# Attention order in steps of two: scores, transposes and applied probabilities of neighbouring steps stand together on PE, with new orders on ACT and DVE

## Chip, core and metric

The kernel runs on one core of a Trainium2 chip. The metric is the device time of one execution in microseconds. It is one program with two blocks: an attention layer (until about 1140 us) and an expert layer behind it.

## What is computed

x holds 64 graphs of 128 nodes with 512 features, adj a 128 x 128 matrix for each. The attention layer has 16 heads of 32 features; adj is used twice as the bias.

```python
h = jnp.maximum(_layernorm(x, axis=-1), 0.0)
x = x + _L0_gnn_ref(h, adj, adj, Wq, Wk, Wv, Wo)
# _L0: q, k, v = split_heads(h @ Wq.T), (h @ Wk.T), (h @ Wv.T)
#      a = einsum('bhnd,bhmd->bhnm', q, k) * 512**-0.5 + 2 * adj
#      p = softmax(a)   (rows that are all zero give p = 0)
#      o = einsum('bhnm,bhmd->bhnd', p, v);  return o @ Wo.T
h = jnp.maximum(_layernorm(x, axis=-1), 0.0)
x = x + _L1_gnn_ref(h, adj, router_w, router_b, expert_w, bn_gamma, bn_beta)
```

The change touches the attention layer alone.

## The kernel before

The attention layer works on two graphs at a time (a pair, 32 pairs). Each graph's 16 heads are four steps of four heads, so a pair has the steps 0 to 7. Every product is made exact in three terms (hi times hi, hi times lo, lo times hi), which is why an operand is copied by ACT (hi) and then subtracted by DVE (lo).

Each engine has an order written out by hand as a string of tokens (`PE_ORDER`, `ACT_ORDER`, `DVE_ORDER`, `POOL_ORDER`, `SP_ORDER`). One pass over the strings is one turn of the loop; a turn starts one S0 after the other. A token is a letter and a step or part. A prime means the pair before; `AHEAD` moves some letters one or two pairs ahead. An engine works strictly in the order of its string and waits at a token for semaphores. The tokens that matter here:

- S: four score matmuls of a step on PE (line 420). L: the scaled scores plus bias, and the negated row maximum, on DVE (lines 356, 361). E: four exponentials on ACT (line 301). B: maximum of the absolute values on DVE (line 364). R: reciprocal and norm on DVE (lines 369, 372). P: the scaling by the norm on POOL (line 268). T: four transposes on PE (line 427). C: their copy on ACT (line 308). W: eight matmuls, 32 columns of weights each, that apply the probabilities on PE (line 436).
- Q0 to Q3: the projections of the next pair on queries (0, 1) and keys (2, 3): 24 matmuls each on PE (line 461, recorded at 43), the copy on ACT (line 319), the subtraction on DVE (line 387). V0, V1: the values, and their copy on ACT (line 325). H: transposes of the normalised input. O: the output projection, with a copy on ACT (line 312) and a subtraction on DVE (line 377). X: the residual on DVE. N and M: layer norm statistics. A: the normalisation on ACT.
- K0 and K1 on the SP queue (lines 244 to 252): 12 transfers each, of 128 KB, that put the queries and keys of a pair's first and second graph from `qk` into `stack`. K0 waits for the last subtraction Q3 of the pair. K1 stands as K1' in the next turn, behind Y1' (a store of 256 KB) and X (a load of 512 KB) in the same queue. Nothing in SP's order is changed.
- `qk` exists once. So ACT's copy Q0 of the next pair waits until all 24 transfers of the pair before have landed:

```python
                        wait(act, qk_projected, 4 * j + k + 1)
                        if k == 0:
                            for g in range(2):
                                wait(act, stacked[g], STACKS * j)
```

S0 waits for K0's landing, S4 for K1's. W0 waits for the subtraction O1' (`o_split`). `bank` has three PSUM banks that Q, V, O and H share by `Q_BANK`, `V_BANK`, `O_BANK` and `H_BANK`; who writes a bank waits until its last reader is done.

Of the kernel before, what the change touches and what calls it, by code (L numbers as in the profile page):

```python
# [32 lines left out]
def wait(engine, semaphore, value):  # L33

    if not isinstance(value, int) or value > 0:
        engine.wait_ge(semaphore, value)
# [31 lines left out]
def attention_layer(nc, ctx, sem, ident, x, adj, weights, x1_dram, expert_w, shared):  # L68
# [14 lines left out]
    def ps(name, shape):  # L83
# [45 lines left out]
    h_transposed, hT_hi_ready, hT_split = sem("h_transposed"), sem("hT_hi_ready"), sem("hT_split")  # L129
    qk_projected, qk_hi_ready, qk_split = sem("qk_projected"), sem("qk_hi_ready"), sem("qk_split")  # L130
    stacked = [sem("stacked0"), sem("stacked1")]
    v_projected, v_copied = sem("v_projected"), sem("v_copied")
# [7 lines left out]
    x1_ready = sem("x1_ready")  # L140
# [5 lines left out]

    PE_ORDER = """S0 W5' T6' H1' O0'
                  S1 T7' W6' Q0  # L150
                  S2 T0 W7' Q1
                  S3 T1 W0 Q2
                  S4 W1 T2 Q3
                  S5 T3 W2 O1'
                  S6 T4 W3 V0
                  S7 T5 W4 H0 V1"""

    ACT_ORDER = """H1' C6' E0
                   C7' E1
                   C0 Q0 O1' E2  # L160
                   V1' Q1 C1 E3
                   Q2 C2 E4
                   Q3 C3 E5
                   C4 A0 O0 E6
                   A1 V0 C5 H0 E7"""

    DVE_ORDER = """R7' L0 H1' B0
                   N0 R0 L1 X0' B1
                   N1 L2 R1 Q0 O1' B2
                   R2 L3 Q1 B3  # L170
                   M R3 L4 Q2 B4
                   R4 Q3 L5 B5
                   L6 R5 X1' B6
                   O0 R6 L7 H0 B7"""

    POOL_ORDER = "P7' D1' P0 P1 P2 P3 G P4 D0 P5 P6"

# [8 lines left out]
             ("sp", PAIRS - 1): "K1' F Z1' Y0' Z0 Y1'",  # L186
             ("act", PAIRS): "C6' F0 C7' O1' F1", ("dve", PAIRS): "R7' F0 X0' O1' X1' F1"}

    Q_BANK, V_BANK, O_BANK, H_BANK = (2, 1, 0, 2), (2, 0), (1, 1), (1, 2)

    def tokens(engine, order, i):

        for t in (START.get((engine, i), order) if isinstance(i, int) else order).split():
            pair = 0 if t[0] in "UF" else i + (AHEAD[engine].get(t[0], 0) - t.endswith("'"))
            if not isinstance(pair, int) or 0 <= pair < PAIRS:
                yield t[0], int(t[1:].strip("'") or 0), pair
# [16 lines left out]
    with nc.Block() as block:  # L213
# [71 lines left out]
        def _(act):  # L285
            def body(i):
                for token, k, j in tokens("act", ACT_ORDER, i):
                    slot = k % 4
# [50 lines left out]
        def _(dve):  # L339
            def body(i):  # L340
                for token, k, j in tokens("dve", DVE_ORDER, i):
                    slot = k % 4
# [67 lines left out]
        @block.tensor  # L410
        def _(pe):
            def body(i):
                for token, k, j in tokens("pe", PE_ORDER, i):
                    g, c, slot = k // C, k % C, k % 4
                    if token == "S":
                        if c == 0:
                            wait(pe, stacked[g], STACKS * (j + 1))
                        wait(pe, logits_ready, STEPS * j + k - 1)
                        for r in range(R):
                            last = nc.tensor.matmul(scores_ps[:, k % 2, r], stack[:, g, r, 0, c], stack[:, g, r, 1, c],  # L420
                                                    start=True, stop=True)
                        last.then_inc(scored, 1)
                    elif token == "T":
                        wait(pe, normed, STEPS * j + k + 1)
                        wait(pe, probT_ready, STEPS * j + k - 1)
                        for r in range(R):
                            last = nc.tensor.transpose(probT_ps[:, k % 2, r], prob[:, slot, r], ident[:])  # L427
                        last.then_inc(transposed, 1)
                    elif token == "W":
                        wait(pe, probT_ready, STEPS * j + k + 1)  # L430
                        if c == 0:
                            wait(pe, v_copied, 2 * j + g + 1)
                            wait(pe, o_split, 2 * j + g)
                        for r in range(R):
                            f = HD * (R * c + r)
                            last = nc.tensor.matmul(o_ps[HD * r:HD * r + HD, c], v[:, g, f:f + HD], probT[:, slot, r],  # L436
                                                    start=True, stop=True)
                        last.then_inc(applied, 1)
                    elif token == "O":
                        wait(pe, o_split, 2 * j + k + 1)  # L440
                        if isinstance(j, int) and j == 0 and k == 0:
                            pe.wait_ge(w_split, 4)

                        if exists(j + 2):
                            wait(pe, *((hT_split, 2 * (j + 2) + 1), (qk_split, 4 * (j + 2) + 2))[k])
                        else:
                            wait(pe, x1_ready, 2 * j + k)
                        exact_product(nc, bank[:, O_BANK[k]], [o_hi[:, c] for c in range(C)], [o_lo[:, c] for c in range(C)],
                                      [w_hi[:, 3, c] for c in range(C)], [w_lo[:, 3, c] for c in range(C)]
                                      ).then_inc(o_projected, 1)  # L450
                    elif token == "Q":
                        if isinstance(j, int) and j == 0 and k % 2 == 0:
                            pe.wait_ge(w_split, k // 2 + 1)

                        wait(pe, *((hT_split, 2 * (j + 1)), (x1_ready, 2 * (j - 2) + 1), (v_copied, 2 * j),
                                   (qk_split, 4 * j + 1))[k])
                        for half in range(2):
                            m = 128 * (2 * (k % 2) + half)
                            last = exact_product(nc, bank[:, Q_BANK[k], 256 * half:256 * half + 256],
                                                 [w_hi[:, k // 2, kc, m:m + 128] for kc in range(KC)],  # L460
                                                 [w_lo[:, k // 2, kc, m:m + 128] for kc in range(KC)],
                                                 [hT_hi[:, kc] for kc in range(KC)], [hT_lo[:, kc] for kc in range(KC)])
                        last.then_inc(qk_projected, 1)
                    elif token == "V":
                        if isinstance(j, int) and j == 0 and k == 0:
                            pe.wait_ge(w_split, 3)
                        wait(pe, qk_split, 4 * j + (4, 3)[k])
                        exact_product(nc, bank[:, V_BANK[k]], [hT_hi[:, kc, k] for kc in range(KC)],
                                      [hT_lo[:, kc, k] for kc in range(KC)],
                                      [w_hi[:, 2, kc] for kc in range(KC)], [w_lo[:, 2, kc] for kc in range(KC)]  # L470
                                      ).then_inc(v_projected, 1)
                    elif token == "H":
                        wait(pe, h_ready, 2 * j + k + 1)

                        wait(pe, *((x1_ready, 2 * (j - 2)), (v_copied, 2 * (j - 1) + 1))[k])
                        for kc in range(KC):
                            last = nc.tensor.transpose(bank[:, H_BANK[k], 128 * kc:128 * kc + 128],
                                                       h[:, k, 128 * kc:128 * kc + 128], ident[:])
                        last.then_inc(h_transposed, 1)

            keep_clock_up(nc, pe, bank[:, 0, 0:128], ident, 40)
            run(pe, body)


def expert_layer(nc, ctx, sem, ident, x1_dram, adj, router_w, router_b, gamma, beta, out_dram, y, shared):
# [83 lines left out]

    PE_ORDER = "Z0 Z1 J P0 P1 Z2 P2 Z3 P3 M"  # L570
    ACT_ORDER = "A2' A3' Z0 P0 A0 A1 Z1 P1 Z2 P2 Z3 P3"
    DVE_ORDER = "M' Y0 Y1 S3' N0 Z0 S0 Z1 S1 Y2 N1 Z2 S2 Y3 J Z3"
    POOL_ORDER = "N0 P0 N1 P1 P2 P3"
# [70 lines left out]
    with nc.Block() as block:  # L644
# [96 lines left out]
        def _(act):  # L741
            def body(i, stays):
                for token, g, group in tokens("act", ACT_ORDER, i):
                    n = G * group + g
# [36 lines left out]
        def _(dve):  # L781
# [18 lines left out]
            def body(i, stays):  # L800
                for token, g, group in tokens("dve", DVE_ORDER, i):
                    n = G * group + g
# [114 lines left out]
        def _(pe):  # L917
            def body(i, stays):
                for token, g, group in tokens("pe", PE_ORDER, i):
                    n = G * group + g  # L920
# [134 lines left out]
```

## Time and profile before

| | |
|---|---|
| median of 3 runs | 1625.91 us (1625.65 to 1627.64) |
| span of the profiled execution | 1624.5 us |
| PE busy | 1414.4 us, 87% |
| weight loads | 1211.5 us, 75% |
| DVE busy | 1220.7 us, 75% |
| ACT busy | 931.5 us, 57% |
| POOL busy | 539.8 us, 33% |
| SP's queue q1 | 218.20 MB, 51.7% of 16 engines |

The shares are means over the span. The slices of the profile show PE at 9 tenths in all slices of the attention layer but the first and the last, DMA between 5 and 6 tenths there, and DVE alone in the last three slices, after the expert layer's matmuls. A wait is named by what came last before it, so a wait that appears rarely and briefly can still be one that is nearly due in each turn.

### The profile page before, as it was taken

How to read it: one execution, taken by the hardware profiler on the slowest of the kernel's cores; microseconds unless marked ns; L12 is line 12 of the kernel's file. 1: busy time of each engine (PE TensorE's matmuls, PEld its weight loads, DVE VectorE, ACT ScalarE, POOL GpSimd, SP SyncE). 2: the span in 40 equal slices, each digit the busy share in tenths (PEclk: the TensorE clock that was granted, in tenths of full speed). 3: DMA queues.
4: the chain of work that ended last, by engine and by line, in shares of the span. 5: the costliest groups of instructions: out<-in, count | busy, mean ns of one | idle time of the engine just before them, and what ended most of it. 6: DMA issues, size and time to landing. Idle time of an engine off the chain costs nothing. (4 is left out here: it accounts for less than half of the span.)

```text
span 1624.5 us, 38099 instructions
## 1 busy us (share of the span) xinstructions
PE 1414.4 (87%) x10994; PEld 1211.5 (75%) x10995; DVE 1220.7 (75%) x2645; ACT 931.5 (57%) x2957; POOL 539.8 (33%) x593
## 2 busy tenths in 40 slices
PE   7999999999999999999999999998799999982000
PEld 6888888888888888888888888886577777772000
DVE  4777777777777777777777777776676667758998
ACT  4677676676766766766766766766455454520000
POOL 0222222223232232222232232222234344425655
PEclk9999999999999999999999999998799999996555
DMA  5955566655666545666555666545243322127963
GB/s 185 249 135 123 135 150 155 151 126 119 147 154 154 142 119 128 150 156 147 137 119 139 151 155 149 123 108 143 92 144 129 129 96 80 46 72 269 342 228 124
DMA packets 144864, 235.52 MB, mean 145 GB/s; under 512 B 17842, under 2 KB 34226, under 8 KB 144818
## 3 DMA queue, kind: packets, MB, share of 16 engines
q1 hardware_dynamic: 136370, 218.20, 51.7%
q10 hardware_dynamic: 8448, 16.78, 2.8%
q8 instruction: 21, 0.34, 0.1%
q14 instruction: 25, 0.20, 0.0%
HBM read 92.30 MB, written 41.94 MB: 83 GB/s over the span
## 5 line engine op out<-in xcount | busy, mean ns | idle before, releaser
L268 POOL TENSOR_TENSOR prob<-prob,norm 128x512 f32<-128x512 f32 x256 | 266.7, 1042 | 789.2 <-DVE norm L372 789.2
L301 ACT ACTIVATE prob<-logits,neg_max 128x128 f32<-128x128 f32 x1024 | 398.1, 394 | 70.0 <-DVE neg_max L361 69.9
L43 PE MATMUL bank<-hT_hi,w_hi 128*128 128x256 f32 x1024 | 303.6, 296 | 2.8 <-DVE hT_lo L405 2.5
L43 PE MATMUL bank<-hT_lo,w_hi 128*128 128x256 f32 x1024 | 291.3, 284 | 0.0
L43 PE MATMUL bank<-hT_hi,w_lo 128*128 128x256 f32 x1024 | 291.1, 284 | 0.0
L356 DVE SCALAR_TENSOR_TENSOR logits<-scores_ps,adj 128x512 f32<-128x512 f32 x256 | 176.7, 690 | 133.6 <-PE scores_ps L420 132.7
L308 ACT ACTIVATE probT<-probT_ps 128x512 f32<-128x512 f32 x256 | 152.7, 596 | 143.0 <-PE probT_ps L427 143.0
L43 PEld LDWEIGHTS bank<-hT_hi,w_hi 128*128 128x128 f32 x1024 | 197.2, 193 | 21.4 <-issue 19.2
L43 PEld LDWEIGHTS bank<-hT_lo,w_hi 128*128 128x128 f32 x1024 | 197.8, 193 | 0.0
L43 PEld LDWEIGHTS bank<-hT_hi,w_lo 128*128 128x128 f32 x1024 | 197.4, 193 | 0.0
L301 ACT ACTIVATION_READ_ACCUMULATOR prob<-logits,neg_max 128x1 f32 x1024 | 195.5, 191 | 0.0
L361 DVE TENSOR_REDUCE neg_max<-logits 128x4 f32<-128x512 f32 x256 | 175.7, 686 | 8.7
L364 DVE TENSOR_REDUCE abs_max<-logits 128x4 f32<-128x512 f32 x256 | 172.9, 676 | 0.0
L427 PE MATMUL probT_ps<-ident,prob 128*128 128x128 f32 x1024 | 163.6, 283 | 4.6 <-POOL prob L268 4.4
L420 PEld LDWEIGHTS scores_ps<-stack 96*128 96x128 f32 x1024 | 146.2, 193 | 16.3 <-DMA stack<-qk 5.6
L420 PE MATMUL scores_ps<-stack 96*128 96x128 f32 x1024 | 145.1, 265 | 4.7 <-DMA stack<-qk 4.7
L43 PE MATMUL out_ps<-w_hi,z_hi 128*128 x256 | 106.8, 417 | 22.2 <-issue 13.4
L427 PEld LDWEIGHTS probT_ps<-ident,prob 128*128 128x128 f32 x1024 | 108.6, 142 | 18.3 <-issue 12.7
L764 ACT ACTIVATE z_hi<-z_ps 128x512 fp32r<-128x512 f32 x64 | 38.1, 598 | 139.1 <-PE out_ps L43 135.0
L736 POOL TENSOR_TENSOR outs<-outs,h x64 | 94.2, 1476 | 58.7 <-DVE outs L904 58.7
L387 DVE TENSOR_TENSOR qk<-bank,qk 128x512 fp32r<-128x512 f32 x128 | 87.8, 686 | 32.2 <-ACT qk L319 32.1
L436 PE MATMUL o_ps<-probT,v 128*32 128x128 f32 x2048 | 109.7, 286 | 0.8 <-ACT probT L308 0.3
(127 smaller groups left out, 2875.2 us busy)
## 6 DMA issues: line engine op xcount, KB each, us to landing
stack<-qk SPq DMA_DIRECT2D x768, 128.0 KB, 2.5
x_in<-in_x SPq DMA_DIRECT2D x32, 512.0 KB, 4.7
x_res<-in_x SPq DMA_DIRECT2D x64, 256.0 KB, 2.8
x_dram<-x_res SPq DMA_DIRECT2D x64, 256.0 KB, 2.8
x_in<-x_dram SPq DMA_DIRECT2D x32, 512.0 KB, 3.7
y<-outs ACTq DMA_DIRECT2D x16, 1024.0 KB, 5.2
out_dram<-outs SPq DMA_DIRECT2D x32, 256.0 KB, 2.0
w_hi<-x_dram SPq DMA_DIRECT2D x8, 1024.0 KB, 9.6
```

What stands on the lines that cost most here:

```text
L43: last = nc.tensor.matmul(out, a, b, start=(n == 0), stop=(n == len(terms) - 1))
L268: nc.gpsimd.tensor_tensor(prob[:, slot], prob[:, slot], norm[:, slot].unsqueeze(2).to_broadcast([N, R, N]), ALU.mult).then_inc(normed, 1)
L301: last = nc.scalar.activation(prob[:, slot, r], logits[:, slot, r], ACT.Exp, bias=neg_max[:, slot, r:r + 1], accum_out=row_sum[:, slot, r: ...
L308: nc.scalar.activation(probT[:, slot], probT_ps[:, k % 2], ACT.Copy).then_inc(probT_ready, 1)
L356: nc.vector.scalar_tensor_tensor(out=logits[:, slot], in0=scores_ps[:, k % 2], scalar=SCALE, in1=adj2[:, k // C].unsqueeze(1).to_broadcast ...
L361: nc.vector.tensor_reduce(neg_max[:, slot], logits[:, slot], X, ALU.max, negate=True).then_inc(neg_max_ready, 1)
L364: nc.vector.tensor_reduce(abs_max[:, slot], logits[:, slot], X, ALU.max, apply_absolute_value=True).then_inc(abs_max_ready, 1)
L387: nc.vector.tensor_tensor(qk[:, lo, :, c:c + 2].rearrange("p g c n -> p c g n"), bank[:, Q_BANK[k]].rearrange("p (c g n) -> p c g n", c=2, ...
L420: last = nc.tensor.matmul(scores_ps[:, k % 2, r], stack[:, g, r, 0, c], stack[:, g, r, 1, c], start=True, stop=True)
L427: last = nc.tensor.transpose(probT_ps[:, k % 2, r], prob[:, slot, r], ident[:])
L436: last = nc.tensor.matmul(o_ps[HD * r:HD * r + HD, c], v[:, g, f:f + HD], probT[:, slot, r], start=True, stop=True)
L736: nc.gpsimd.tensor_tensor(out, out, coef_rows[1][:, bass.ds(e, 1)], ALU.add).then_inc(shifted, 1)
```

## The change

The orders of PE, ACT and DVE in the attention layer are rewritten. On PE two S stand together, then two T and two W of earlier steps; before, each S, T and W stood alone between larger blocks. Q2 and Q3 swap their banks (2 and 0 instead of 0 and 2), and the waits of Q2, Q3, V0 and V1 follow. POOL's and SP's orders, the unrolled orders at the start and the end, and all instructions stay.

```diff
-    PE_ORDER = """S0 W5' T6' H1' O0'
-                  S1 T7' W6' Q0
-                  S2 T0 W7' Q1
-                  S3 T1 W0 Q2
-                  S4 W1 T2 Q3
-                  S5 T3 W2 O1'
-                  S6 T4 W3 V0
-                  S7 T5 W4 H0 V1"""
-
-    ACT_ORDER = """H1' C6' E0
-                   C7' E1
-                   C0 Q0 O1' E2
-                   V1' Q1 C1 E3
-                   Q2 C2 E4
-                   Q3 C3 E5
-                   C4 A0 O0 E6
-                   A1 V0 C5 H0 E7"""
-
-    DVE_ORDER = """R7' L0 H1' B0
-                   N0 R0 L1 X0' B1
-                   N1 L2 R1 Q0 O1' B2
-                   R2 L3 Q1 B3
-                   M R3 L4 Q2 B4
-                   R4 Q3 L5 B5
-                   L6 R5 X1' B6
-                   O0 R6 L7 H0 B7"""
+    PE_ORDER = """S0 S1 H1' O0' T6' T7' W4' W5' Q0
+                  S2 S3 Q1 T0 T1 W6' W7' Q2
+                  S4 S5 Q3 T2 T3 W0 W1 O1'
+                  S6 S7 V0 T4 T5 W2 W3 H0 V1"""
+
+    ACT_ORDER = """H1' E0 C6' E1 C7'
+                   Q0 E2 Q1 C0 E3 C1 O1' V1'
+                   Q2 E4 Q3 C2 E5 C3
+                   A0 A1 E6 C4 E7 O0 H0 V0 C5"""
+
+    DVE_ORDER = """R7' L0 L1 H1' B0 R0 X0' B1 N0 R1
+                   Q0 L2 L3 B2 R2 Q1 B3 N1 R3
+                   Q2 L4 L5 O1' B4 R4 Q3 M B5 R5
+                   L6 L7 X1' B6 R6 B7 O0 H0"""
...
-    Q_BANK, V_BANK, O_BANK, H_BANK = (2, 1, 0, 2), (2, 0), (1, 1), (1, 2)
+    Q_BANK, V_BANK, O_BANK, H_BANK = (2, 1, 2, 0), (2, 0), (1, 1), (1, 2)
...
-                        wait(pe, *((hT_split, 2 * (j + 1)), (x1_ready, 2 * (j - 2) + 1), (v_copied, 2 * j),
-                                   (qk_split, 4 * j + 1))[k])
+                        wait(pe, *((hT_split, 2 * (j + 1)), (x1_ready, 2 * (j - 2) + 1), (qk_split, 4 * j + 1),
+                                   (v_copied, 2 * j))[k])
...
-                        wait(pe, qk_split, 4 * j + (4, 3)[k])
+                        wait(pe, qk_split, 4 * j + (3, 4)[k])
```

## Rows read from the trace of the kernel before

**Rows 1.** Busy time by stretch: engines with counts, granted clock, DMA share, GB/s.
```profile
80.00:1160.00 1080.00, 1067.78 (x8596) 916.73 (x8594) 817.84 (x1832) 743.85 (x2587) 309.45 (x377) 0.99 0.58 138
1116.00:1124.00 8.00, 7.63 (x46) 5.43 (x47) 5.34 (x14) 5.94 (x24) 2.45 (x4) 0.50 0.50 157
1200.00:1260.00 60.00, 55.12 (x410) 45.93 (x408) 41.37 (x124) 30.10 (x54) 27.18 (x29) 1.00 0.37 127
```

**Rows 2.** Timeline of SP's queue: start, length, line, transfers, count, merged.
```profile
612.47 7.70 SPq L249 DMA_DIRECT2D stack<-qk  x12
...
646.94 7.70 SPq L249 DMA_DIRECT2D stack<-qk  x12
...
656.43 7.69 SPq L249 DMA_DIRECT2D stack<-qk  x12
...
681.42 7.68 SPq L249 DMA_DIRECT2D stack<-qk  x12
...
716.08 7.68 SPq L249 DMA_DIRECT2D stack<-qk  x12
```

**Rows 3.** Timeline of ACT: copy Q0 in two turns; in brackets the wait.
```profile
634.65 0.60 ACT L319 ACTIVATE qk<-bank 128x512 fp32r<-128x512 f32 x1 [0.45 <-DMA stack<-qk]
...
704.11 0.60 ACT L319 ACTIVATE qk<-bank 128x512 fp32r<-128x512 f32 x1 [0.96 <-DMA stack<-qk]
```

**Rows 4.** DMA issues, 663.3 to 664.1: count, KB each, us to landing.
```profile
stack<-qk SPq DMA_DIRECT2D x2, 128.0 KB, 4.0
```

**Rows 5.** What copies of line 319 waited for, 400 to 1100: us, times.
```profile
  DMA stack<-qk: 2.7, 5
```

**Rows 6.** Timeline of ACT, 635 to 640, first instructions of E, V1', Q1, E.
```profile
635.63 0.41 ACT L301 ACTIVATE prob<-logits,neg_max 128x128 f32<-128x128 f32 x1
...
637.17 0.58 ACT L325 ACTIVATE v<-bank 128x512 f32<-128x512 f32 x1
637.65 0.59 ACT L319 ACTIVATE qk<-bank 128x512 fp32r<-128x512 f32 x1
...
639.13 0.40 ACT L301 ACTIVATE prob<-logits,neg_max 128x128 f32<-128x128 f32 x1 [0.41 <-DVE neg_max L361]
```

**Rows 7.** Timeline of DVE, 635 to 647: Q, O, R, L, Q and Q3.
```profile
635.28 0.69 DVE L387 TENSOR_TENSOR qk<-bank,qk 128x512 fp32r<-128x512 f32 x1 [0.36 <-ACT qk L319]
635.89 0.68 DVE L377 TENSOR_TENSOR o_lo<-o_ps,o_hi 128x512 fp32r<-128x512 f32 x1
...
637.30 0.18 DVE L369 RECIPROCAL inv_sum<-row_sum 128x4 f32<-128x4 f32 x1
...
637.68 0.69 DVE L356 SCALAR_TENSOR_TENSOR logits<-scores_ps,adj 128x512 f32<-128x512 f32 x1
...
639.01 0.68 DVE L387 TENSOR_TENSOR qk<-bank,qk 128x512 fp32r<-128x512 f32 x1
...
646.14 0.69 DVE L387 TENSOR_TENSOR qk<-bank,qk 128x512 fp32r<-128x512 f32 x1 [0.86 <-ACT qk L319]
```

**Rows 8.** Timeline of PE, 602 to 609: groups S, T, W and first Q matmuls.
```profile
602.35 0.56 PE L420 MATMUL scores_ps<-stack 96*128 96x128 f32 x4
602.74 0.62 PE L427 MATMUL probT_ps<-ident,prob 128*128 128x128 f32 x4
603.29 0.43 PE L436 MATMUL o_ps<-probT,v 128*32 128x128 f32 x8
603.65 0.38 PE L43 MATMUL bank<-hT_hi,w_hi 128*128 128x256 f32 x1
603.87 0.28 PE L43 MATMUL bank<-hT_lo,w_hi 128*128 128x256 f32 x1
...
606.62 0.56 PE L420 MATMUL scores_ps<-stack 96*128 96x128 f32 x4
...
607.46 0.66 PE L427 MATMUL probT_ps<-ident,prob 128*128 128x128 f32 x4
607.88 0.36 PE L43 MATMUL bank<-hT_hi,w_hi 128*128 128x256 f32 x1
```

## The prediction

> **What bounds the kernel now.** I read the busy time by stretch first. Between 80 and 1160 us PE is busy 1067.8 of 1080 us at the full clock, so in the attention layer PE is the bound and nobody else is: DVE has 817.8, ACT 743.9 [rows 1]. The turns are equal: K0's first transfer is issued at 612.47 and again at 646.94, that is 34.47 us per turn [rows 2]. One turn is one pair. 29 turns are of this full kind; the first, the last two and the expert layer are other stretches.
>
> A busy PE is only half of the reading. The second question is what is nearly late. ACT's copy Q0 carries a bracket "<-DMA stack<-qk", 0.45 us in one turn and 0.96 us in another [rows 3]; there were 5 such waits, 2.7 us in all, in the 20 turns from 400 to 1100 [rows 5]. So the transfers of K1 land about when ACT comes to Q0, and there is a second loop beside PE's: K0 and K1 issued, landed, Q0 copied, the chain of ACT and DVE up to the subtraction Q3, K0 issued again.
>
> Its first half is the transfers. K0's 12 issues take 7.70 us, 0.64 each; K1's first comes 9.49 us after K0's first (646.94 to 656.43), as Y1' and X stand between, and takes 7.69 again [rows 2]. The last issue is near 663.5 and lands 4.0 later [rows 4], at 667.5: 20.6 after K0's start. In the turns in which ACT waited, it started 22.18 (612.47 to 634.65) and 22.69 (681.42 to 704.11) after K0's start [rows 2, 3]. Most turns are of the first kind; I take 21.2 on the mean, with 20.6 and 22.7 as ends.
>
> Its second half, from ACT's Q0 to K0's issue, was 646.94 - 634.65 = 12.29, and 716.08 - 704.11 = 11.97 in the turn with the later landing [rows 2, 3]. That last turn took 716.08 - 681.42 = 34.66, 0.19 over PE's 34.47: so here the second loop just ruled, 22.69 + 11.97. On the mean it needs at most 21.2 + 11.97 = 33.2, and has at least 1.3 us to spare. This is the margin that the change must be held against.
>
> **The change on PE.** No instruction is added or removed. A T takes 0.55 from its start to the W behind it, but 0.42 to a Q behind it (607.46 to 607.88); W takes 0.36 and the first Q matmul behind it 0.22, where the other 23 take (606.62 - 603.87) / 23 = 0.12 each [rows 8]. So an entry into the W kind costs 0.13, and leaving it some 0.1 to 0.2 more. Eight visits a turn become four. S after S and W after W are not in the trace: I take 0.3 for a visit saved, with 0.13 (the entry alone) and 0.4 as ends. That is 1.2 us a turn (0.5 to 1.6), and PE's turn becomes 33.3 (32.9 to 34.0). T behind an O, a Q or a V is new too; S stands there at 0.39 per group [rows 8], which is inside these ends.
>
> **The change on ACT and DVE.** Here the loop through the transfers must be walked again, since its second half is exactly the part of the orders that is rewritten. Prices, start to start: E 1.54 (635.63 to 637.17), a copy 0.48 (637.17 to 637.65) [rows 6]; L 1.33 (637.68 to 639.01), a subtraction 0.60 (635.28 to 635.89, B taken as the same), R 0.38 (637.30 to 637.68), ACT's copy Q0 to DVE's subtraction Q0 0.63 (634.65 to 635.28), L's start to E's start 1.45 (637.68 to 639.13), subtraction Q3 to K0's issue 0.80 (646.14 to 646.94) [rows 2, 3, 6, 7].
>
> The new orders read, for ACT, Q0 E2 Q1 C0 E3 C1 O1' V1' Q2 E4 Q3, and for DVE, Q0 L2 L3 B2 R2 Q1 B3 N1 R3 Q2 L4 L5 O1' B4 R4 Q3. Counted from ACT's Q0 at 0: DVE's Q0 at 0.63, L2 at 1.23, E2 at 2.68, ACT's Q1 4.22, C0 4.70, E3 5.18 (L3 was done in time), C1 6.72, O1' 7.20, V1' 7.68, Q2 8.16. DVE has by then done L3, B2, R2, Q1, B3, N1 and R3 (until about 7.2) and waits for this Q2: it comes at 8.79, L4 at 9.39, L5 10.72, O1' 12.05, B4 12.65, R4 13.25, Q3 at 13.63. E4 starts at 10.84 and ends near 12.4, so neither R4 nor ACT's Q3 is late. Q3 to K0 adds 0.80: **14.43 us from ACT's Q0 to K0's issue**, where the old orders managed 11.97.
>
> What made it longer can be named. In the new order DVE's Q3 stands behind L4, L5, O1', B4 and R4 with nothing of them done before Q2, and ACT's Q2 stands behind two E, two C, O1' and V1', with E2 itself behind the L2 that comes only after DVE's Q0. In the old order one L stood between neighbouring subtractions Q.
>
> Is PE late anywhere in this chain? From the end of its Q0, PE needs S2 S3 Q1 T0 T1 W6' W7' Q2, about 0.8 + 2.95 + 0.9 + 0.6 + 2.97 = 8.2 us with the spacings above, as much as ACT's 8.16. As ACT's Q0 will wait for the transfers and come some 2 us behind PE's Q0, PE is ahead. T0, T1 need P0, P1, done long before. G on POOL now stands before P4 with M behind Q3 on DVE, so P4 starts near 16.2, but T4 comes only near 20: hidden. A0 and A1 wait for the same G near 16.3, and E6 behind them needs an L6 that is not ready before 17 either. SP's X is behind A1 (near 17.7), K0's issues last until 14.43 + 7.7 = 22.1: hidden.
>
> **The sum.** The loop through the transfers: 21.2 to the landing, about 0.1 to ACT's Q0, 14.43 to K0: 35.7 us a turn. PE needs 33.3 in the same time. What is late next is PE itself: its Q3 waits for ACT's copy V1' (bank 0), its W0 for DVE's O1', together about 2.4 us idle a turn. So the loop rules, and each full turn grows by 35.7 - 34.47 = 1.26 us; 29 of them give 36.5. The ends: the first full landing comes while the expert weights are loaded (about +1), the last pair has no X before its K1 (about -1), behind it the paired order may save or cost a microsecond or two: 0 in sum, 3 either way. The expert layer is not touched. The profiled execution would have 1624.5 + 36.5 = 1661.0 of span; the median lies 1.4 above the span, so 1662 us.
>
> **A rule weighed.** The row first: the stack transfers of 128 KB follow each other at 0.64 us [rows 2], which is 205 GB/s, and no transfer of this stretch shows that this is the queue's issue or the engines' rate. The Trainium skill, page "DMA: Bandwidth & Descriptors", section "Where 436 GB/s comes from", puts the ceiling for SBUF to SBUF at 435 GB/s; as an estimate from that page a transfer would take 0.30 us, 24 of them 7.2 instead of 15.4, and the loop would be near 28 us, PE the bound again, with the time of the first rival below. The trace doesn't agree, and the row decides.
>
> **Rival 1, faster: PE stays the bound.** If the stretch from K0's first issue to K1's landing were shorter, 33.4 - 0.1 - 14.43 = 18.9 us or less, the gain of PE would come through. It would need each transfer at about 0.54 instead of 0.64, or a chain on ACT and DVE that is 2.3 us shorter than walked. For it: the landings themselves vary by 2 us. Against it: every turn read has 20.6 or more [rows 2 to 4], and strict orders leave no short cut. PE's turn would be 33.4 (W0 waits for O1' by 0.1 even then): 29 x -1.07 = -31, so 1595. The skill's ceiling would bring just this. Chance 0.10.
>
> **Rival 2, no change: the two cancel.** With the landing at 20.6 or a little less throughout and a chain 0.6 shorter, a turn is 34.5: 1626. Chance 0.06.
>
> **Rival 3, slower still: the clock.** PE now idles twice in a turn. After an idle time in the last pair the granted clock was 0.50 for a whole stretch (1116 to 1124), while at 55.12 busy of 60 us in the expert layer it stayed at 1.00 [rows 1]. The new turn would have 33.3 of 35.7, 93%, like the latter. If the clock fell for part of each turn, PE would need 2 to 4 us more per turn, of which the 2.4 idle hide most; up to 1 us would remain: 1662 + 29 = 1691. Chance 0.07.
>
> **How the numbers follow.** The forecast has 0.77. Its own range: 20.6 instead of 21.2 gives 35.1 a turn and 1645; 21.7 gives 36.2 and 1676; 0.2 us of error in the chain adds 6 either way, the ends 3: 1638 to 1685. Within it the forecast has some 0.72; the clock's case with a mild fall reaches to 1690. So the range is 1638 to 1690, with rival 1 and most of rival 2 left out. Faster by over 0.2% has rival 1 and a little of rival 2: 0.12. Within 0.2% (3 us, about what a measurement of this kernel can tell from no change): 0.04. Slower: 0.84.
>
> **What would show it.** Right: turns of about 35.7 between K0's first issues; a bracket "<-DMA stack<-qk" of 1.5 us or more at ACT's Q0 in each turn; about 14.4 from that copy to K0's first issue; PE idle before Q3 (for ACT's V copy) and before W0 (for DVE's o_lo); W groups of 16 and PE busy about 33.3 a turn. Wrong: turns under 34.5 with PE without idle time (rival 1); a distance from K0's first issue to ACT's Q0 under 20 with a wait; a granted clock under 0.95 in the attention layer (rival 3).

## The result and the profile after

The changed kernel takes 1671.03 us (median of 4 runs, 1668.74 to 1672.96) against 1626.78 for the kernel before beside it: 1.027 times as long, 95% interval 1.0255 to 1.0284. Forecast were 1662, between 1638 and 1690.

The first lines of the page of the changed kernel:

```profile
span 1667.0 us, 38044 instructions
## 1 busy us (share of the span) xinstructions
PE 1399.7 (84%) x10994; PEld 1228.2 (74%) x10995; DVE 1211.5 (73%) x2645; ACT 912.3 (55%) x2957; POOL 537.9 (32%) x593
```

PE is busy for 15 us less than before, with the same 10994 matmuls, and the span is 42.4 us longer. So PE's work did shrink, and something else set the time. All shares and rows here are of one profiled execution, the shortest of the four. SP's queue (start, length, line, transfers) shows a turn, from one first issue of K0 to the next:

```profile
778.42 7.69 SPq L237 DMA_DIRECT2D stack<-qk  x12
787.91 7.65 SPq L237 DMA_DIRECT2D stack<-qk  x12
...
814.12 7.70 SPq L237 DMA_DIRECT2D stack<-qk  x12
```

814.12 - 778.42 = 35.70, where [rows 2] had 34.47; K1 still comes 9.49 behind K0. In the same turn ACT's copies Q0 and Q3 and DVE's subtractions Q0 and Q3 (line 307 answers to 319 of before, 375 to 387):

```profile
799.52 0.60 ACT L307 ACTIVATE qk<-bank 128x512 fp32r<-128x512 f32 x1 [3.50 <-DMA stack<-qk]
...
811.99 0.57 ACT L307 ACTIVATE qk<-bank 128x512 fp32r<-128x512 f32 x1
```

```profile
800.15 0.69 DVE L375 TENSOR_TENSOR qk<-bank,qk 128x512 fp32r<-128x512 f32 x1 [4.13 <-ACT qk L307]
...
813.32 0.69 DVE L375 TENSOR_TENSOR qk<-bank,qk 128x512 fp32r<-128x512 f32 x1
```

These rows show the two halves of the loop. From K0's first issue to ACT's Q0, 799.52 - 778.42 = 21.10, with 3.50 us of waiting for transfers at its end, where [rows 3] had 0.45 and 0.96 in single turns. From ACT's Q0 to K0's next issue, 814.12 - 799.52 = 14.60, where [rows 2, 3] gave 12.29 and 11.97. Over the 27 turns from the third to the 29th the means are 21.07 to the landing, 0.08 to the copy and 14.60 to K0: 35.75.

PE in the same turn, and its busy time between the two S0 (engines in the order of [rows 1]):

```profile
788.65 1.01 PE L408 MATMUL scores_ps<-stack 96*128 96x128 f32 x8
...
807.92 0.38 PE L43 MATMUL bank<-hT_hi,w_hi 128*128 128x256 f32 x1 [1.41 <-ACT v L313]
...
812.46 0.64 PE L424 MATMUL o_ps<-probT,v 128*32 128x128 f32 x16 [0.53 <-DVE o_lo L365]
...
824.35 1.01 PE L408 MATMUL scores_ps<-stack 96*128 96x128 f32 x8
```

```profile
788.65:824.35 35.70, 33.76 (x281) 30.00 (x280) 26.05 (x60) 23.41 (x84) 9.85 (x12) 1.00 0.59 136
...
1143.10:1188.00 44.90, 30.57 (x217) 23.36 (x215) 24.47 (x48) 23.41 (x80) 9.63 (x10) 0.81 0.32 93
```

In this turn PE stands idle exactly twice, before Q3 (for the copy V1', 1.41) and before W0 (for the subtraction O1', 0.53), 1.94 us together; S and W come in groups of 8 and 16 matmuls. Over the turns from 95 to 1090 us its idle time is 1.65 us a turn.

Where the 42.4 us of span lie: 37.2 between the first S0 and the 31st (1032.8 before, 1070.0 after), -0.4 in the turn behind it, +6.8 from the last S0 to the last subtraction of the layer (the tail: 37.6 before, 44.3 after, to the subtraction's start), -1.3 in the expert layer. The 6.8 were not forecast. The last turn before, for comparison with the second line above:

```profile
1106.18:1144.34 38.16, 30.97 (x209) 22.79 (x207) 24.41 (x49) 24.17 (x80) 9.73 (x10) 0.82 0.37 105
```

PE's busy time is nearly the same in both (30.97 and 30.57); it stands idle for twice as long. The longest of these idle times, in PE's timeline of the changed kernel:

```profile
1165.76 0.65 PE L424 MATMUL o_ps<-probT,v 128*32 128x128 f32 x16
1170.89 0.79 PE L43 MATMUL bank<-w_hi,o_hi 128*128 128x512 f32 x1 [4.48 <-DVE o_lo L365]
1176.17 1.04 PE L415 MATMUL probT_ps<-ident,prob 128*128 128x128 f32 x8
```

O0' now stands before T6' and T7'. In the last turn PE waits 4.48 us for DVE's o_lo and then works through O0', with the transposes of the last two steps queued behind. How much of the 6.8 this order costs is tested at the end of the experiments.

### The profile page after: what moved, and what is told of

Read it like the earlier page. It is cut to its first block and busy times, and to the rows that moved or that the text cites. A ratio compares the mean times of both kernels' runs of the same rounds, so it can differ in the third digit from the quotient of the medians.

```text
span 1667.0 us, 38044 instructions
## 1 busy us (share of the span) xinstructions
PE 1399.7 (84%) x10994; PEld 1228.2 (74%) x10995; DVE 1211.5 (73%) x2645; ACT 912.3 (55%) x2957; POOL 537.9 (32%) x593
## 5 line engine op out<-in xcount | busy, mean ns | idle before, releaser
L43 PE MATMUL bank<-hT_lo,w_hi 128*128 128x256 f32 x1024 | 295.6, 289 | 0.0
L43 PEld LDWEIGHTS bank<-hT_hi,w_hi 128*128 128x128 f32 x1024 | 201.6, 197 | 55.0 <-ACT v L313 39.1
L43 PEld LDWEIGHTS bank<-hT_hi,w_lo 128*128 128x128 f32 x1024 | 202.3, 198 | 0.0
L43 PEld LDWEIGHTS bank<-hT_lo,w_hi 128*128 128x128 f32 x1024 | 202.3, 198 | 0.0
L408 PEld LDWEIGHTS scores_ps<-stack 96*128 96x128 f32 x1024 | 130.7, 193 | 13.3 <-DMA stack<-qk 6.7
L415 PE MATMUL probT_ps<-ident,prob 128*128 128x128 f32 x1024 | 134.0, 273 | 4.1 <-POOL prob L256 4.1
L408 PE MATMUL scores_ps<-stack 96*128 96x128 f32 x1024 | 130.7, 271 | 6.7 <-DMA stack<-qk 6.7
L307 ACT ACTIVATE qk<-bank 128x512 fp32r<-128x512 f32 x128 | 75.0, 586 | 111.3 <-DMA stack<-qk 97.5
L415 PEld LDWEIGHTS probT_ps<-ident,prob 128*128 128x128 f32 x1024 | 117.4, 141 | 13.5 <-POOL prob L256 5.0
L43 PE MATMUL bank<-w_hi,o_hi 128*128 128x512 f32 x256 | 108.5, 424 | 7.1 <-DVE o_lo L365 7.1
```

The costliest lines, as they stand in the source:

```text
L43: last = nc.tensor.matmul(out, a, b, start=(n == 0), stop=(n == len(terms) - 1))
L307: nc.scalar.activation(qk[:, t, :, c:c + 2].rearrange("p g c n -> p c g n"), bank[:, Q_BANK[k]].rearrange("p (c g n) -> p c g n", c=2, g=2 ...
```

## The experiments

**A transfer more.** Two kernels get a 13th transfer of 128 KB behind K1's twelve, and ACT's Q0 and S4 wait for it too. Nobody reads what it brings.

```diff
+    STACKS_OF = (STACKS, STACKS + 16)
...
+    spare = sb("spare", [HD, 2, C, N], F32R)
...
+                        if g == 1:
+                            sp.dma_start(spare[:].bitcast(F32).rearrange("p t c n -> p t (c n)"),
+                                         qk[0:HD, Q_HI:K_HI + 1:K_HI - Q_HI, 1].bitcast(F32).rearrange("p t c n -> p t (c n)"),
+                                         ).then_inc(stacked[g], 16)
```

> The changed kernel with one more transfer of 128 KB behind K1's twelve, into a spare tile that nobody reads; ACT's copy Q0 and S4 wait for it too. Theory (the loop from K0's issue over K1's landing to ACT's Q0 and back sets the turn): the landing comes 0.64 us later, the price of one transfer in the queue, and all of it goes through, so a turn takes 36.4 instead of 35.75 and the kernel 29 x 0.64 = 19 us more, 1690. Rival (the new orders of PE, ACT and DVE wait for each other and would take 35.7 without any transfer): the copy has room, no change, 1671.

> The kernel before with the same additional transfer. Theory: its loop has 1.3 us to spare on the mean, so the 0.64 are mostly hidden; only turns whose landing is late by itself pass something on, 0.1 to 0.3 us a turn on the mean, 1629 to 1635. Rival (transfers cost bandwidth or queue time wherever they stand): 19 us more as in the changed kernel, 1645.

The changed kernel took 1688.94 us, 18 more than its 1671.03 in the earlier comparison and 1.038 times the kernel before (1.036 to 1.0399). The landing came at 21.62 instead of 21.07 on the mean, the turn was 36.32 instead of 35.75: 0.55 in, 0.57 out. The kernel before, with the same addition, took 1629.13 beside 1627.11, ratio 1.0012 (1.0002 to 1.0021), and its turn 34.51 instead of 34.49. The same transfer costs 18 us in one kernel and 2 in the other. It isn't bandwidth that is paid but the place in the loop; both times are what the theory expects, and both rivals fall. In the kernel before, three of the 27 turns grew by more than 0.1 us (34.60, 34.79 and 35.02): those with the latest landings, as expected.

**Four transfers less.** K1 leaves out the third term of the scores (query hi times key lo) for the second graph of each pair; its rows of the stack are set to zero once, and PE's work stays.

```diff
+    STACKS_OF = (STACKS, STACKS * 2 // 3)
...
-                        for s, (a, b) in enumerate(((Q_HI, K_HI), (Q_LO, K_HI), (Q_HI, K_LO))):
+                        for s, (a, b) in enumerate(((Q_HI, K_HI), (Q_LO, K_HI), (Q_HI, K_LO))[:3 - g]):
```

> The changed kernel with 8 instead of 12 transfers for K1: the third term of the scores (query hi times key lo) is left out for the second graph of each pair, its rows of the stack stay zero; all PE instructions stay. Theory: the landing comes 4 x 0.64 = 2.56 us earlier, the loop needs 33.2, and PE's own turn shows itself, 33.4 to 33.8 where it was 34.47 before; 29 x 2.1 = 61 us less, 1610, and thereby faster than the kernel before. Rival (orders wait for each other): 1671 as it is; or PE's grouping brings nothing: a turn of 34.5, 1634.

> The kernel before with the same 8 transfers for K1 (third term of the second graph left out). Theory: PE is the bound there, so nothing changes, 1625 to 1627 with turns of 34.47, but the waits of ACT's Q0 for the transfers disappear. Rival (the transfers were a part of the turn before already): some us less, up to 2.5 a turn.

The changed kernel fell to 1620.25 us, 0.9954 of the kernel before (0.9938 to 0.9971). 51 us went where 61 were expected. The turn was 34.09 on the mean, and 33.74 to 33.78 in 18 of the 27 turns. In eight of the others the landing came late, 19.4 us or more behind K0, and the loop set the turn again; the longest of them, from 95.4 us on, took 37.9. The changed kernel has such a turn at the same place (37.9), and the cause is open: the expert weights, four transfers from 44.3 us on, had landed by 60 us here and by 62 there. PE's waits from 400 to 800 us (us in total, times, longest):

```profile
PE o_ps L429 <- DVE o_lo L368: 3.6, 12, 0.5
PE bank L43 <- ACT v L316: 0.6, 1, 0.6
```

The wait for V1' is gone there in all turns but one; the one for O1', 0.3 a turn, is left. So in most turns PE is the bound again, at 0.7 under the old 34.47, but the mean turn is only 0.4 under it, and the tail is 45.0 us, 7.5 more than before: that is why the end gain is small.

In the kernel before, leaving out the same transfers changed nothing: 1626.44 beside 1627.11, ratio 0.9993 (0.9983 to 1.0004), turns of 34.48. What the copies Q0 to Q3 waited for there, 400 to 1000 us:

```profile
L322 ACT ACTIVATE qk<-bank x70: 592/600/603, 399.7 to 989.9; 128x512 fp32r<-128x512 f32 x70
its engine sat idle before it (us, times) until:
  PE bank L43: 25.0, 36
```

The line "DMA stack<-qk" of [rows 5] is no longer there, and the time is the same: before the change these waits cost nothing.

**The other half of the loop.** In the changed kernel DVE's Q3 goes ahead of B4 and R4.

```diff
-                   Q2 L4 L5 O1' B4 R4 Q3 M B5 R5
+                   Q2 L4 L5 O1' Q3 B4 R4 M B5 R5
```

> The changed kernel with one move in DVE's order: the subtraction Q3 stands before B4 and R4 instead of behind them. Theory (the chain of ACT and DVE from the copy Q0 to K0's issue, 14.60 us, is the second half of the loop): ACT's copy Q3 is ready in time, so Q3 and K0 come 0.6 us earlier and the whole of it shows, a turn of 35.15 and 29 x 0.6 = 17 us less, 1654. Rival (the landing of the transfers has its own pace and the chain only fills the time): no change, 1671.

It took 1652.78 us, 1.0146 times the kernel before (1.0125 to 1.0166), 18 us less than the changed kernel; between the two profiled executions it is 11.3 (1655.7 against 1667.0). The chain was 13.99 on the mean instead of 14.60 and the turn 35.32 instead of 35.75: 0.61 less in the chain, of which 0.18 went back into a later landing (21.25 instead of 21.07). So the turn fell by 0.43, not by the 0.6 expected. In the trace not every turn had the same chain: 13.87 in most, 14.50 in some. Such a turn, its granted clock (last column but two) and PE's wait in it:

```profile
726.00:732.00 6.00, 4.32 (x24) 4.18 (x24) 4.27 (x9) 3.92 (x15) 1.04 (x1) 0.72 0.00 0
```

```profile
728.13 0.58 PE L43 MATMUL bank<-hT_hi,w_hi 128*128 128x256 f32 x1 [1.68 <-ACT v L313]
...
732.58 1.04 PE L415 MATMUL probT_ps<-ident,prob 128*128 128x128 f32 x8
```

Behind 1.68 us of waiting the first Q3 matmul takes 0.58 instead of 0.38, and Q3 as a whole 4.45 us (728.13 to 732.58) instead of the 2.97 from 807.92 on in the changed kernel: a part of it ran at the lower of the two clock levels. ACT's copy Q3 comes 0.6 late by that, and here, where Q3 stands first on DVE, this goes into the loop. In the changed kernel's own trace there were six such dips in the steady turns, and its chain was 14.60 in them too, as B4 and R4 covered the delay.

**PE's part alone.** PE's new order and banks, with the ACT and DVE orders of before.

```diff
-    ACT_ORDER = """H1' E0 C6' E1 C7'
-                   Q0 E2 Q1 C0 E3 C1 O1' V1'
...
+    ACT_ORDER = """H1' C6' E0
+                   C7' E1
+                   C0 Q0 O1' E2
...
+    DVE_ORDER = """R7' L0 H1' B0
+                   N0 R0 L1 X0' B1
+                   N1 L2 R1 Q0 O1' B2
...
```

> PE's new order and banks alone, ACT and DVE in the orders of the kernel before. Theory: the chain from ACT's Q0 to K0 is short again (near 12.3 us), so the transfers no longer set the turn; but ACT's C0 stands before Q0 and T0 now comes only behind Q1, so Q0 comes at 13.4 after S0, PE's Q2 waits some 1 us for the subtraction Q0, and late steps wait for each other: a turn near 35.0, 1645, between 1632 and 1665. Rival (the grouping on PE is what costs): 1671 or more, with PE busy for longer in a turn than the 33.3 to 33.4 that PE's own work takes in the changed kernel.

It took 1676.79 us, ratio 1.0307 (1.0285 to 1.0329): outside the 1632 to 1665 that I gave it. ACT (two rows) and PE's weight loads, 400 to 800 us, 11 turns:

```profile
765.46 0.60 ACT L304 ACTIVATE probT<-probT_ps 128x512 f32<-128x512 f32 x1 [2.49 <-PE probT_ps L423]
765.95 0.59 ACT L315 ACTIVATE qk<-bank 128x512 fp32r<-128x512 f32 x1
```

```profile
PEld bank L43 <- DVE qk L383: 8.8, 22, 0.6
PEld probT_ps L423 <- POOL prob L264: 8.1, 22, 0.6
...
PEld bank L473 <- ACT x_in L325: 6.4, 11, 0.6
PEld scores_ps L416 <- DVE logits L352: 5.8, 11, 0.6
```

The first half of the expectation held: Q0 came at 13.74 after S0 (752.21), behind C0's wait for T0, the chain to K0 was 12.21, and Q0 waited for no transfer, as the landing was 2.7 us ahead on the mean. The turn was 35.6 all the same. Six waits of 0.4 to 0.6 us stand in each turn; the four kinds above add up to 29.1 us in 11 turns. My guess of 1 us at Q2 and little else was the miss: projections, transposes of probabilities and of the input, and scores each wait a little, and the tail was 13 us longer than before (50.5 against 37.6). Both signs of the rival came too: over 1671, and in the turn from S0 (752.21 to 787.76) PE is busy for 34.48 us, more than the 33.4. This run alone doesn't refute it; the next one does, where the same order on PE takes 33.52 us a turn. So this kernel is slow for another reason than the changed one, and the old ACT and DVE orders were no way out.

**The chain made short.** The changed kernel, DVE's order alone rewritten in two places:

```diff
-                   Q0 L2 L3 B2 R2 Q1 B3 N1 R3
-                   Q2 L4 L5 O1' B4 R4 Q3 M B5 R5
+                   L2 Q0 L3 B2 R2 Q1 B3 N1 R3
+                   Q2 L4 O1' L5 Q3 B4 R4 M B5 R5
```

> The changed kernel with a new order on DVE alone: L2 before the subtraction Q0 (it needs no transfer), and Q2 L4 O1' L5 Q3 B4 R4 in the place of Q2 L4 L5 O1' B4 R4 Q3. Theory: E2 is ready when the copy Q0 is done, the chain shrinks by 0.6 + 0.7 at the end and by up to 0.6 at the start, to 12.1 to 12.8, the loop needs 33.3 to 33.9, and W0 no longer waits for O1'. PE becomes the bound with 33.4 to 33.8 a turn; 29 x 2.1 = 61 us less than the changed kernel, 1610, and less than the kernel before. Rival (something else than this chain holds the turn): 1640 to 1671.

It took 1603.15 us, 0.9852 of the kernel before (0.9834 to 0.9869), 68 less than the changed kernel and 7 less than expected. A turn of its PE, and ACT's copy Q0 in that turn:

```profile
675.30:708.82 33.52, 33.52 (x281) 29.91 (x280) 26.13 (x60) 23.30 (x84) 9.85 (x12) 1.00 0.63 144
```

```profile
686.24 0.60 ACT L307 ACTIVATE qk<-bank 128x512 fp32r<-128x512 f32 x1 [3.57 <-DMA stack<-qk]
```

PE is busy for 33.52 of 33.52 us: it is the bound, with 33.53 from turn to turn, 0.94 less than before the change. And ACT still waits 3.57 us for the transfers, more than the 3.50 in the changed kernel, and it costs nothing now: the chain behind it took 11.61 to 13.52, whatever the landing left, and 12.59 on the mean. Three tokens changed places in this run (L2, O1' and Q3); what each of them brings by itself was tested for Q3 alone, above.

**The tail.** As the last kernel, with an order of its own for PE's last turn.

```diff
-    START = {("act", -2): "U0 A0 A1 H0", ("act", -1): "H1' U1 U2 Q0 Q1 U3 Q2 Q3 A0 A1 V0 H0",
+    START = {("pe", PAIRS): "T6' T7' W4' W5' O0' W6' W7' O1'",
+             ("act", -2): "U0 A0 A1 H0", ("act", -1): "H1' U1 U2 Q0 Q1 U3 Q2 Q3 A0 A1 V0 H0",
```

> As l2_first, and in the last, unrolled turn PE does T6' T7' W4' W5' before O0' instead of behind it. In the changed kernel the stretch from the last S0 to the last subtraction of the layer took 44.95 us, 6.8 more than before, with PE waiting 4.48 us for DVE before O0' while T6 and T7 stood behind it. Theory: half of this comes back, 3 to 4 us less than l2_first. Rival (the tail is set by the granted clock and the copies): within 1 us of l2_first.

It took 1601.60 us (1599.79 to 1603.25) beside 1603.15 (1602.2 to 1604.79): 0.9835 of the kernel before (0.9818 to 0.9852). In the traces the tail was 39.9 us instead of 42.7 (44.3 in the changed kernel, 37.6 before, all to the start of the last subtraction). The trace shows 2.8 of the 3 to 4 expected; the medians differ by 1.6, between theory and rival, with intervals that overlap, so for the time of the whole this gain is not shown. PE still stands idle at the same place, for 3.69 us, now before T6' and for POOL's scaled probabilities: so O0' ahead of T6' and T7' is only a part of the longer tail, and the rest stays open. This version has the lowest median, 26 us under the kernel before.

## Why the prediction was right

**The bound and its margin.** That the landing of K1 was nearly late before, with some 1.3 us to spare, is what the whole forecast rested on. The 27 turns before have 21.20 to the landing on the mean; with 0.08 to the copy and the shortest chain, 11.97, that is 33.25, or 1.2 to spare. The added and left-out transfers show it: in the kernel before nothing changes in one direction, and 2 us in the other.

**The transfers' half.** Taken at 21.2, measured 21.07 to the landing. Adding one transfer moved it by 0.55 and leaving out four by 2.09, 0.52 each. That is less than the 0.64 between two issues [rows 2], which both expectations had taken as the price: the last issue moved by 0.61 and 2.55, but the time from it to the landing moved the other way, from 4.37 to 4.31 and 4.84.

**The chain.** Walked as 14.43, measured 14.60: the copy Q1 came 4.31 behind Q0 instead of 4.22, Q3 on DVE 13.79 instead of 13.63. The turn was 35.75 for the forecast 35.7. q3_first shortened this half and the time followed, by 0.43 of the 0.61 a turn.

**PE's own turn.** Forecast 33.3 out of 32.9 to 34.0. l2_first, where PE never waits, has 33.53. Put down to the four visits to the W kind alone, the 0.94 us less are 0.24 a visit, where the forecast took 0.3 from [rows 8]; S and T were regrouped as well, and no run tests them apart. Start to start, a step into a W group and a step out of one take 0.20 us each in the traces of both kernels, and a step within one 0.02; the kernel before has sixteen of the long steps a turn and l2_first eight. The Trainium skill, page "TensorEngine Tiling (Array Packing)", section "Key Properties", says that a change of the tiling mode drains the engine. The 0.20 us steps agree with it. PE's two idle places were named rightly; together they were 1.94 in the turn shown and 1.65 on the mean instead of 2.4.

**The rule on the DMA rate.** K0's twelve issues took near 7.7 us in the steady turns of every run, 0.64 a transfer or 205 GB/s. The ceiling of 435 GB/s that the Trainium skill gives (page "DMA: Bandwidth & Descriptors", section "Where 436 GB/s comes from") was not reached in any run. Rival 1 needed the landing at 18.9 instead of 21.2 and did not come. short_after made that case by hand, and its mechanism is real: with the landing 2.1 us earlier the kernel gained instead of losing.

**The terms that were off.** The ends were put at 0 with 3 either way and were near 6: the mis-sized term is the last turn, +6.8, in which O0' stands ahead of T6' and T7' on PE and waits 4.48 us; the order of its own in l2_tail brought 2.8 back. I had said that the paired order "may save or cost a microsecond or two" without walking it. The forecast put about 1 us on the first full landing, beside the loading of the expert weights; the turn that grew most, from 34.9 to 37.9 us, is the third, which begins at 97.6 us, when they have all landed. Why its landing was late (23.24 behind K0) stays open. The 30 turns up to the 31st S0 grew by 37.2 us where 29 x 1.26 = 36.5 were forecast, and the expert layer was 1.3 shorter. The median lies 4.0 over the profiled span instead of 1.4. These make up nearly all of the 9 us between 1662 and 1671; the steady turns have hardly a part in it.

**The clock.** From 111 to 1109 us the granted clock of the changed kernel was 0.99 on the mean, so rival 3 did not come. Its mechanism exists in small: short dips behind PE's idle time. In the changed kernel B4 and R4 on DVE covered them; in q3_first they cost up to 0.6 in a turn, and in extra_after, in two of the 27 turns, the chain was 15.39 instead of 14.60 behind a longer dip.

## What to carry to other kernels

When one engine is the bound, look for loops over other engines and transfers that close within the same turn, and find from the rare late turns how much they have to spare; a brief wait that appears in a quarter of the turns is the sign of it. A new order is then to be walked along such a loop from the shared buffer's release to its next fill, as that is where one operation ahead of another counts in full. A wait's length says nothing of its cost: 3.5 us at the same copy set the time in one kernel and were free in the next, with DVE's order rewritten in two places between them.

## What the hardware showed beside that

Transfers from SBUF to SBUF of 128 KB were issued 0.64 us apart in the steady turns of every kernel, 205 GB/s. Each transfer added or left out moved the last landing by 0.52 to 0.55 us in the changed kernel. PE's clock fell for a short time after short idle times, in stretches that are busy otherwise: after 1.68 us in the turn shown (0.72 granted over the 6 us), and in the changed kernel after six idle times of 1.35 to 2.0 us. After others it did not, such as the 1.41 us before 807.92 and one of 2.35 us; what decides between them stays open.
